# Adding up expert rows with four 64x64 tiles of TensorE: two accumulator banks, a fold by a stacked identity, and a new order of the pieces

## The reference, cut to what matters

```python
scores, pk = jax.lax.top_k(all_scores, TOPK)            # 8 experts for each token and each of 4 heads
indices = jnp.take_along_axis(all_indices, pk, axis=-1)
down = down_embed[indices]
up = up_embed[indices]
w = jnp.einsum('btd,bthkd->bthk', hidden_states, down)
w = jax.nn.silu(w) * jax.nn.softmax(scores, axis=-1)
experts_states = jnp.einsum('bthk,bthkd->btd', w, up)
mlp = jax.nn.silu(hidden_states @ Wg.T) * (hidden_states @ Wu.T) @ Wd.T
return mlp + experts_states
```

## Time and profile before

| what | value |
|---|---|
| median of 3 runs | 4052.93 us (4036.28 to 4060.89) |
| profiled execution, its own time | 4046.25 us |
| its span, first to last instruction | 4044.5 us |
| instructions | 75813 |
| mean granted TensorE clock | 0.972 of full speed |
| TensorE (PE) busy | 3814.3 us, 94% |
| VectorE (DVE) busy | 2827.7 us, 70% |
| ScalarE (ACT) busy | 2275.8 us, 56% |
| GpSimd (POOL) busy | 2242.3 us, 55% |

### The profile page before, as it was taken

How to read it: one execution, slowest core, us unless ns; L and a number is a source line. 1 busy time by engine, 2 the same in 40 slices (tenths; PEclk the granted TensorE clock), 3 DMA queues, 4 the chain that set the end, 5 groups by cost and what they waited for, 6 DMA issues and landing times.

```text
span 4044.5 us, 75813 instructions
## 1 busy us (share of the span) xinstructions
PE 3814.3 (94%) x25720; PEld 2763.9 (68%) x25720; DVE 2827.7 (70%) x9152; ACT 2275.8 (56%) x6594; POOL 2242.3 (55%) x2091
## 2 busy tenths in 40 slices
PE   7699999897679999999999999999999999999998
PEld 5577777675346777777777777777777777777766
DVE  4577787775367777777777777777777777777763
ACT  2333443343256666666666666666666666666663
POOL 1555565566266555565565565556555556556540
PEclk8899999999789999999999999999999999999999
DMA  3655555567100001000100001000010000010000
GB/s 118 154 155 144 148 154 141 153 164 201 47 1 6 7 8 35 31 12 6 39 16 27 7 6 37 17 29 4 7 39 14 29 7 27 16 31 14 5 7 27
DMA packets 110543, 210.95 MB, mean 52 GB/s; under 512 B 22321, under 2 KB 71505, under 8 KB 108625
## 3 DMA queue, kind: packets, MB, share of 16 engines
q0 software_dynamic: 40960, 134.25, 12.7%
q1 hardware_dynamic: 69056, 71.71, 5.5%
q10 hardware_dynamic: 144, 0.13, 0.0%
HBM read 191.39 MB, written 2.10 MB: 48 GB/s over the span
## 4 chain that ended last, share of the span: by engine, by line
PE 67%; issue 2%; DVE 2%; POOL 1%; ACT 1%; DMA 0%; SPq 0%; DVEq 0%; POOLq 0%; ACTq 0%
PE pj L1594 23%; PE pj L1674 12%; PE y_ps L1657 8%; PE y_ps L1683 6%; PE sc L1622 5%; PE o_ps L1648 4%; PE tp L1633 4%; PE tp L1602 4%; PE tp L1572 1%; POOL l_qk_rot L1535 1%; ACT l_probs L1753 0%; DVE l_probs L1890 0%; POOL l_r_q L1540 0%; DVE l_qk_cos L1866 0%; POOL l_r_k L1540 0%
## 5 line engine op out<-in xcount | busy, mean ns | idle before, releaser
L1594 PE MATMUL pj<-w_qkv,l_xT 128*128 128x512 f32 x2304 | 1063.1, 598 | 7.2 <-DMA l_qk_gain<-in_gains 3.6
L1535 POOL TENSOR_TENSOR l_qk_rot<-l_qk_cos,l_qk_sin 128x512 f32<-128x512 f32 x384 | 564.8, 1471 | 840.5 <-DVE l_qk_sin L1869 555.7
L382 POOL DMA_INDIRECT f_rows<-in_emb,f_expert x512 | 514.6, 1005 | 382.2 <-PE facc L601 175.0
L1594 PEld LDWEIGHTS pj<-w_qkv,l_xT 128*128 128x128 f32 x2304 | 413.5, 191 | 385.8 <-issue 375.9
L1753 ACT ACTIVATE l_probs<-l_probs,l_low 128x128 f32<-128x128 f32 x1536 | 594.0, 391 | 2.4 <-DVE l_low L1890 0.6
L1674 PE MATMUL pj<-l_xnT,l_w 128*128 128x256 f32 x2112 | 510.9, 387 | 2.2 <-issue 1.2
L1861 DVE TENSOR_REDUCE l_ss<-l_qk_sq 128x8 f32<-128x512 f32 x384 | 261.6, 681 | 324.9 <-ACT l_qk_sq L1740 173.3
L1890 DVE CUSTOM_DVE_ANT_0 l_probs<-sc,l_shut,l_r_q 128x128 f32<-128x128 f32 x1536 | 440.2, 344 | 54.4 <-PE tp L1633 46.7
L1718 ACT ACTIVATE l_qk_raw<-pj 128x512 f32<-128x512 f32 x384 | 227.0, 591 | 434.6 <-PE pj L1594 419.6
L1674 PEld LDWEIGHTS pj<-l_xnT,l_w 128*128 128x128 f32 x2112 | 383.9, 190 | 65.0 <-issue 17.4
L1657 PE MATMUL y_ps<-w_o,l_oT 128*128 128x256 f32 x1536 | 341.2, 380 | 3.5 <-ACT l_oT L1718 3.5
(11 more groups left out here) (324 smaller groups left out, 7164.6 us busy)
## 6 DMA issues: line engine op xcount, KB each, us to landing
w_qkv<-in_L_ffn_Wqkv SPq DMA_DIRECT2D x12, 1024.0 KB
l_w<-in_ff_w SPq DMA_DIRECT2D x6, 1408.0 KB, 6.1
f_rows<-in_emb,f_expert POOLq DMA_INDIRECT x512
w_o<-in_L_ffn_Wo SPq DMA_DIRECT2D x6, 1024.0 KB
w_qkv<-in_L_ffn_Wqkv SPq DMA_DIRECT2D x12, 512.0 KB
l_xf<-l_stream SPq DMA_DIRECT2D x48, 128.0 KB
l_xf<-l_stream SPq DMA_DIRECT2D x48, 127.0 KB
l_w<-in_ff_w SPq DMA_DIRECT2D x6, 768.0 KB, 4.9
```

Of the source, the lines that this page charges most:

```text
L382: pool.indirect_dma_start(rows[:, j % RH, k, :], None, dram["emb"], bass.IndirectOffsetOnAxis(ap=expert[:, n % 2, at:at + 1], axis=0)).the ...
L1535: pool.tensor_tensor(qk_rot[:, i % ROTS, :], qk_cos[:, b, :], qk_sin[:, b, :], ALU.add).then_inc(rotated if s == 0 else pool_front, 1)
L1594: last = pe.matmul(pj[b][:, :], xT[:, k, t * P:(t + 1) * P], w_qkv[:, k, s * INNER + c * 512:s * INNER + (c + 1) * 512], start=(k == 0), s ...
```

## The change

HP = 64. Each 128 tokens are two halves of 64.

- **diag** is 128x64 a slot in place of 128x128: pairs is an identity of 64x64 twice, one below the other, and c_diag (same line of code, same count) scales it. Rows 0 to 63 hold the diagonal of the first half's tokens, rows 64 to 127 that of the second's.
- **c_up** becomes eight matmuls of 64x64 by 64x256 in place of four of 128x128 by 128x256. Expert slots k and k + 1 are done together: for slot k, half i goes to output partitions of half i; for slot k + 1, to those of the other half. Half i always writes bank acc[i]. So four tiles of the array, two by rows and two by columns, have work of their own.
- **acc** is two banks, acc[0] and acc[1], and the ring has BANKS = 6.
- **c_y** becomes 16 matmuls of 128x64 by 128x256 in place of 8 of 128x128: columns for half j into acc[j].
- **c_fold** is new: ScalarE copies both banks to SBUF (two copies of 128x512, into the buffer of e_p, which now has 128 partitions), TensorE multiplies each by pairs (two matmuls of 128x64 by 128x512 into a bank of the ring), which adds each half's two parts, and VectorE's c_add takes that bank. c_y and c_up of the next batch wait for ScalarE's copies (c_copied) in place of c_add.
- GpSimd makes pairs at the start: a fill and two selects.
- **The tables** of all five engines are new.

```diff
-        ("c_up14", -5), ("c_up15", -5), ("c_m7", -4), ("c_y0", -4), ("c_up0", -4), ...
+        ("c_up15", -5), ("c_fold", -5), ("c_m7", -4), ("c_y0", -4), ("c_up0", -4), ...
...
-        ("e_ctx", -5), ("e_mask", -4), ("b_ctx", -2),
+        ("b_ctx", -1), ("e_mask", -3), ("e_ctx", -3),
...
-    BANKS = 7
+    BANKS = 6
...
+        pairs = sb("pairs", [P, HP])
...
-        diag = sb("diag", [P, 2, HALF, P])
+        diag = sb("diag", [P, 2, HALF, HP])
...
-        e_p = sb("e_p", [4 * NB, H4, SEQ])
+        e_all = sb("e_p", [P, H4, SEQ])
+        e_p = e_all[0:4 * NB, :, :]
...
+        folding = e_all[:, :, :].rearrange("p (i t) d -> p i t d", i=2)
...
-        acc = ctx.enter_context(nc.psum_tensor("facc", [P, TILES, D], F32))
+
+        acc = [ctx.enter_context(nc.psum_tensor(f"facc{i}", [P, TILES, D], F32)) for i in range(2)]
...
@@ c_y @@
-                            last = pe.matmul(acc[:, t, :], mT[:, i, t * P:(t + 1) * P], c_wd[:, i, :], ...)
+                            for j in range(2):
+                                last = pe.matmul(acc[j][j * HP:(j + 1) * HP, t, :], mT[:, i, t * P + j * HP:t * P + (j + 1) * HP], c_wd[:, i, :], ...)
...
@@ c_up @@
-                    wait(pe, c_added, n)
+                    wait(pe, c_copied, n)
...
-                    for k in range(HALF):
-                        last = pe.matmul(acc[:, j // (HALVES // TILES), :], diag[:, j % 2, k, :], rows[:, j % RH, k, D:2 * D],
-                                         start=(first and k == 0), stop=(final and k == HALF - 1))
+                    for k in range(0, HALF, 2):
+                        for s in range(2):
+                            for i in range(2):
+                                rows_at, out_at = slice(i * HP, (i + 1) * HP), slice((i ^ s) * HP, (i ^ s) * HP + HP)
+                                last = pe.matmul(acc[i][out_at, j // (HALVES // TILES), :], diag[rows_at, j % 2, k + s, :], rows[rows_at, j % RH, k + s, D:2 * D], ...)
...
+            def c_fold(n):
+                pe.wait_ge(c_copied, n + 1)
+                s = Slot("c_fold", n)
+                wait(pe, s.taken, s.before)
+                for i in range(2):
+                    last = pe.matmul(s.bank[i * HP:(i + 1) * HP, :], pairs[:, :], folding[:, i, :, :].rearrange("p t d -> p (t d)"), start=True, stop=True)
+                last.then_inc(ps_full, 1)
...
@@ ScalarE @@
-                        last = F(diag[:, j % 2, k, :], ident[:, :], ACT.Copy, scale=coef[:, j % 2, k:k + 1])
+                        last = F(diag[:, j % 2, k, :], pairs[:, :], ACT.Copy, scale=coef[:, j % 2, k:k + 1])
...
+            def c_fold(n):
+                act.wait_ge(m_used[0], n + 1)
+                act.wait_ge(m_used[1], n + 1)
+                act.wait_ge(rows_used, HALVES * (n + 1))
+                wait(act, ps_full, Slot("e_pT", n - 1).full if n > 0 else 0)
+                for i in range(2):
+                    last = F(folding[:, i, :, :], acc[i][:, :, :], ACT.Copy)
+                last.then_inc(c_copied, 1)
```

More of the change, by code:

```diff
@@ L55, in first_layers @@
     SCALE = 1.0 / 8.0
+    HP = P // 2
     ORDER = {}
     ORDER["tensor"] = [
[6 rows of a table removed]
-        ("e_s1", -5), ("c_up7", -4), ("c_up8", -4), ("a_k", -1), ("c_up9", -4), ("e_v", -5), ("e_cT", -4), ("e_pT", -5), ("a_q", -1), ("e_o", -5),
-        ("a_z", -1), ("e_y", -5), ("b_hT", -2), ("c_hT", -3), ("e_u", -5), ("c_q0", -3),
+        ("c_s0", -4), ("c_s2", -4), ("b_hT", -3), ("c_s1", -4), ("c_s3", -4), ("c_up11", -5), ("b_cT", -3), ("a_v", -2), ("c_up12", -5), ("e_k", -5),
+        ("c_m0", -4), ("c_m1", -4), ("c_m2", -4), ("c_m3", -4), ("b_g", -3), ("c_m4", -4), ("c_up13", -5), ("c_m5", -4), ("c_up14", -5), ("c_m6", -4),
+        ("c_up15", -5), ("c_fold", -5), ("c_m7", -4), ("c_y0", -4), ("c_up0", -4), ("d_hT", -5), ("a_o", -2), ("d_k", -5), ("d_q", -5), ("a_y", -2),
[3 rows of a table added]
+        ("a_q", -1), ("c_up7", -4), ("e_v", -5), ("c_up8", -4), ("c_y1", -4), ("e_pT", -5), ("c_up9", -4), ("e_o", -5), ("a_z", -1), ("e_y", -5),
+        ("c_hT", -3), ("e_cT", -4), ("e_u", -5), ("c_q0", -3), ("c_q1", -3), ("c_up10", -4),
@@ L68, in first_layers @@
     ]
     ORDER["scalar"] = [
[6 rows of a table removed]
-        ("c_diag8", -4), ("c_diag9", -4), ("b_cT", -2), ("e_exp", -5), ("e_v", -5), ("e_cT", -4), ("e_pT", -5), ("a_q", -1), ("e_o", -5),
-        ("c_tanh10", -4), ("c_diag10", -4), ("e_y", -5),
+        ("c_hT", -4), ("c_diag10", -5), ("e_cT", -5), ("c_tanh11", -5), ("c_tanh12", -5), ("c_q0", -4), ("c_diag11", -5), ("c_q1", -4),
+        ("c_tanh13", -5), ("b_cT", -3), ("c_diag12", -5), ("b_hT", -3), ("e_k", -5), ("a_exp", -2), ("a_v", -2), ("c_mtanh0", -4), ("c_diag13", -5),
[5 rows of a table added]
@@ L78, in first_layers @@
+        ("c_diag9", -4), ("e_pT", -5), ("e_o", -5), ("c_tanh10", -4), ("e_y", -5),
     ]
     ORDER["vector"] = [
[4 rows of a table removed]
[L84 to L86 removed]
@@ L361, in start @@
                 fill(zeros[:, :], 0.0)
+                fill(pairs[:, :], 0.0)
+                for at in (0, HP):
+                    pool.wait_ge(set_step, made[0])
+                    pool.affine_select(out=pairs[:, :], in_=pairs[:, :], pattern=[[-1, HP]], base=-at, channel_multiplier=1,
+                                       compare_op=ALU.not_equal, fill=1.0).then_inc(set_step, 1)
+                    made[0] += 1
                 pool.wait_ge(set_step, made[0])
@@ L589, in down @@
                         for i in chunks:
-                            last = pe.matmul(acc[:, t, :], mT[:, i, t * P:(t + 1) * P], c_wd[:, i, :], start=(first and t == 0 and i == chunks[0]),
-                                             stop=(final and t == TILES - 1 and i == chunks[-1]))
+                            for j in range(2):
+                                last = pe.matmul(acc[j][j * HP:(j + 1) * HP, t, :], mT[:, i, t * P + j * HP:t * P + (j + 1) * HP], c_wd[:, i, :],
+                                                 start=(first and t == 0 and i == chunks[0]), stop=(final and t == TILES - 1 and i == chunks[-1]), skip_group_check=True)
                     last.then_inc(m_used[half], 1)
@@ L597, in add_rows @@
                     first, final = ACC_ORDER[0] == f"c_up{j}", ACC_ORDER[-1] == f"c_up{j}"
-                    wait(pe, c_added, n)
+                    first_up = [piece for piece in ACC_ORDER if piece.startswith("c_up")][0] == f"c_up{j}"
+                    wait(pe, c_copied, n)
                     pe.wait_ge(diag_made, HALVES * n + j + 1)
-                    for k in range(HALF):
-                        last = pe.matmul(acc[:, j // (HALVES // TILES), :], diag[:, j % 2, k, :], rows[:, j % RH, k, D:2 * D],
-                                         start=(first and k == 0), stop=(final and k == HALF - 1))
+                    for k in range(0, HALF, 2):
+                        for s in range(2):
+                            for i in range(2):
+                                rows_at, out_at = slice(i * HP, (i + 1) * HP), slice((i ^ s) * HP, (i ^ s) * HP + HP)
+                                last = pe.matmul(acc[i][out_at, j // (HALVES // TILES), :], diag[rows_at, j % 2, k + s, :], rows[rows_at, j % RH, k + s, D:2 * D],
+                                                 start=((first_up if s else first) and k == 0), stop=(final and k == HALF - 2), skip_group_check=True)
                     last.then_inc(rows_used, 1)
                 return add_rows
+            def c_fold(n):
[5 more added lines that the diff above has]
+                last.then_inc(ps_full, 1)
             def d_q(n):
@@ L737, in _ @@
             do.update({f"c_up{j}": c_up(j) for j in range(HALVES)})
+            do["c_fold"] = c_fold
             do.update({"a_q": a_q, "a_k": a_k, "a_v": a_v, "a_z": a_z, "a_o": a_o, "a_y": a_y, "b_cT": b_cT, "b_g": b_g, "b_gt": b_gt,
@@ L1082, in c_m @@
                 return gate
-            def c_add(n):
-                dve.wait_ge(m_used[0], n + 1)
-                dve.wait_ge(m_used[1], n + 1)
-                dve.wait_ge(rows_used, HALVES * (n + 1))
-                x = xall[:, n, :, :]
-                V.tensor_tensor(x, acc[:, :, :], x, ALU.add).then_inc(c_added, 1)
             def d_top_(n):
```

22 lines of the change are left out of this document (13 added, 9 removed), and 35 rows, old and new, of the table ORDER.

## The result

The change measured 4082.7 us (median of 11 runs, 4067.0 to 4102.0) against 4054.0 for before (11 runs): ratio 1.0079, 95% interval 1.0064 to 1.0095. It is slower by 0.8%, where 1.4% faster was forecast, and lies above the range. The profiled execution took 4091.8 us, its span is 4090.1.

The account below looks back on a forecast made before the run. TensorE leads, with gathers, VectorE and the gather-to-c_up chain close behind. Terms sum to -7.2 us a batch, -57.6 over eight, plus 2.6 of tail: -55, giving 3998 us on the runs' footing, range 3945 to 4055.

Parts of the forecast that it names:

- c_up: TensorE's c_up matmuls: four small tiles run at once, 1.73 us becomes 1.05, 10.9 us less a batch.
- c_y: TensorE's c_y: 32 records, two tiles at once, work stays 3.46 us a piece; shape changes add 0.4 a batch.
- c_fold on TensorE: The new fold's 4 matmul records add 1.05 us of TensorE work a batch, changes of tile shape included.
- c_diag: ScalarE's diagonal copies, 64 columns shorter: 0.18 us less per four, taken as -0.5 us a batch.
- The ratio 0.65: Share of TensorE's 9.5 us saving a batch that shortens the period: -6.2 us, bounds -2.2 to -7.1.
- The wait at the accumulator: TensorE waits 1.6 us at c_fold for ScalarE's copies, replacing c_y0's 1.65 for c_add: 0, bounds -0.5 and +1.6.
- c_add later: VectorE's c_add gets its bank 2.6 us later, after copies and fold: +1.0 us a batch, bounds 0 to +2.6.
- The rest of the tables, and six banks: 0: Reordered tables and the ring's lost bank together cost nothing; bounds -3 and +3.9 us a batch.
- the context's 1.5 a batch: TensorE's wait for b_ctx's transfer mostly disappears as its load is released earlier: -1.5 us a batch, bounds 0 to -1.7.
- The ends: At the last batch nothing covers the fold, so the tail grows 2.6 us; GpSimd's setup at the start costs 0.
- the stall of TensorE's queue at c_fold: Rival: TensorE stands 1.6 us at c_fold and 3.9 at the ring: +5.9 a batch, 4103 us; chance 0.08.
- The rival of four tiles that go in turn because they accumulate: c_up's four tiles run one after another, 3.65 us each, +31 a batch, 4350 us; chance 0.03.

Follow-up runs that it names:

- h4: The change with c_fold one row later on TensorE, behind c_m7, faster kind: 3971.4 us, 0.9937 of before.
- h3: The change with whole 128x128 tiles and one accumulator, copies and fold kept, faster kind: 3996.3 us, 1.0005 of before.
- h2: Before's whole tiles, no fold, with the change's tables and six banks, faster kind: 3968.8 us, 0.9936 of before.
- h1: The change itself, unaltered, run again on the faster kind: 3958.5 us, 0.9915 of before.
- e6: Before with six banks in place of seven and nothing else, slower kind: 4065.9 us, 1.0040 of before.
- i1: Before's whole tiles, no fold, with the change's tables and six banks, slower kind: 4050.9 us, 1.0007 of before.
- e5: Before's whole tiles, no fold, with the change's tables and seven banks, slower kind: 4041.6 us, 0.9979 of before.
- f1: The change itself, unaltered, run again on the faster kind: 3958.7 us, 0.9911 of before.
- f3: The change's tiles and fold in before's tables, six banks, faster kind: 4009.4 us, 1.0046 of before.
- fourth group: Runs of before, h1, h2, h3 and h4 on one chip of the faster kind; the change took 3958.5 us there, 0.9915 of before.
- f4: The change with each c_up matmul starting its own sum, expert rows not added up, faster kind: 3961.3 us, 0.9908 of before.

## Why the prediction was wrong, step by step

- **c_up.** Right. 16 records in 1.09 us, four starting within 0.02 us and each four 0.216 to 0.27 after the four before, where I had them evenly 0.054 apart. With c_y, tiles were forecast at -10.5 us of TensorE a batch; at full clock it is -10.0 (h4 against h3).
- **c_y.** Right: 32 records in 3.67 us, two tiles at once, weight loads hidden. The rule that I weighed from the Trainium skill ("TensorE: Matmul & The Clock Gate", Part 3: Packing small matmuls) would have made it 7.9; the trace disagrees.
- **c_fold on TensorE.** 1.05 forecast, 1.5 measured at full clock. Tiles and fold together take 8.5 out at full clock (105.9 in h2, 97.4 in h1), where 9.5 was forecast.
- **c_diag.** Right: the four of a group take 1.06 us in place of 1.28, 0.21 less, where 0.18 was forecast.
- **The ratio 0.65.** Right in size where TensorE's work does fall, in the full stretches of the faster kind: h3 to h1 the period goes down 6.6 us (110.1 to 103.5) for 8.5 to 10.0 of work, 0.66 to 0.78. Over all eight batches it is 4.5 a batch: the sum took the gain of a full stretch eight times.
- **The wait at the accumulator.** The step that failed: "One wait of 1.6 takes the place of one of 1.65: 0". On the faster kind TensorE does wait 1.34, but no other wait goes away for it: period less TensorE's busy time rises from 0.7 (h2) to 2.3 (h3). On the slower kind, which the forecast was for, it waits 7.6 us. I had put 0.2 us for "the last record to get through", from no row at all; it was 5.5 to 7.7 in six of the eight batches. My bound of +1.6 lay far below. Against before, TensorE's idle time in a full stretch grew by 8.2 us (7.8 to 16.0), and some 6 of that is the wait at c_fold (7.6) less the one at c_y0 that it replaced (1.65 in four batches of five).
- **c_add later.** 2.6 forecast for the chain, 2.47 in h1; in after it is 610.05 - 600.54 = 9.5. The price of +1.0 a batch was perhaps too low even on the faster kind: h4, where c_fold and c_add come 0.5 later, is 1.6 us a batch slower than the change. That the delay is what costs it was not shown.
- **The rest of the tables, and six banks: 0.** Two effects of opposite sign. The lost bank costs 0.3 to 0.4% on the slower kind (e6; i1 less e5), 11 to 16 us in all, 1.4 to 2.0 a batch, inside my bound of +3.9. The new tables give 0.2% there, where the context's 1.5 a batch alone would be 0.3%; the two together, forecast at -1.5 a batch, come to +0.07% (i1), nothing. On the faster kind tables and bank together give 0.6% with whole tiles. With tiles and fold the tables alone give 1.35% (f1 less f3, both with six banks). Whether they suit the tiled kernel better cannot be said, since the bank's price on this kind was not measured; if it were 0.4% as on the other, 1.0% would stand against 1.35%.
- **The clock.** No term of mine held it. Around the wait of 7.48 us at c_fold the granted clock was 0.51 (605.10 to 612.00), with 1.00 on both sides; in full stretches it is 0.91 against 0.96. TensorE's busy time fell by 1.8 us there, where at full clock the same change takes 8.5 out.
- **The ends.** The last c_add comes 2.54 us after the last c_up, as forecast. I had also written that the tail would be near 55; but it is cut at c_add, so the fold cannot lengthen it, and it is 52.6, as before:

```profile
1075.04 1.62 PE L617 MATMUL facc<-f_rows,f_diag 64*64 64x256 f32 x16 [0.15 <-ACT f_diag L829]
1076.86 1.08 ACT L839 ACTIVATE f_e_p<-facc 128x512 f32<-128x512 f32 x2 [1.97 <-PE facc L617]
...
1079.20 0.69 DVE L938 TENSOR_TENSOR x_all<-fp,x_all 128x512 f32<-128x512 f32 x1 [5.41 <-PE fp L627]
```

In sum, -7.2 a batch was forecast. On the faster kind the change gives 34.8 us in the fourth group, -4.3 a batch: tables and bank -3.2, fold +3.4, tiles -4.5 (the table's per cent of 3993 us, over eight batches). On the slower kind the stretches grow by 6.4, and stay above the 116 that I had named as the sign of being wrong. Of the rivals, the stall of TensorE's queue at c_fold came nearest (4103 us, +5.9 a batch), at a chance of 0.08: right in place, near in size by luck. It had 1.6 us at c_fold, where 7.6 was seen, and 3.9 for the ring, where the bank costs 1.4 to 2.0. What held TensorE there was the late result of c_up15, which the rival did not have. The rival of four tiles that go in turn because they accumulate is refuted by the records and by f4. Two sums of mine were wrong as well. The bounds of the terms, added up, are -15.2 and +5.9 a batch, 3934 to 4103 us, and not 3965 to 4030; the wider range would have held the result. And four in turn would be +32 a batch with c_y and fold, not +37.

**What stays open.** Why results come late on one kind of chip, and why more so with small tiles. The traces of that kind also lack signals: the semaphore that counts full banks shows 397 of its 456 rises in after and 373 of 448 in before, all 456 in h1; hence "<-remote" and "<-issue" where h1 names TensorE. So the missing rises go with the kind of chip and not with small tiles. Late results would follow if records of the profile held engines up. The Trainium skill ("NOTIFIC — the notification-queue block", section 7.1, on overflow) describes such a block: it can stall what feeds it, and its inner queues hold the producer back rather than lose a record. Missing rises would not follow from that; the same section has another mode, in which a full ring discards new records. A c_up of small tiles is 32 instructions of TensorE in 1.1 us in place of 16 in 1.9. No run here tells this from another cause. The wait at c_fold is some 6 of the 8.2 us of idle time that a full stretch gained, but that its removal would bring them back was not shown: the one kernel that moved c_fold fell on the faster kind. The price of the seventh bank on the faster kind, and which rows of the tables carry their 0.6%, were not tried.

## What to carry to other kernels

Before pricing a handover at 0.2 us, measure in the trace of before how long after a matmul's last record its reader starts, place by place: here a third of the waiting gathers began late, up to 8 us after the record, and the change, which adds a handover with nothing queued in between, paid 7.6 us a batch at it. TensorE's 8.5 us less of work were worth something only where it kept its clock and was not made to stand. And run the change itself beside every variant on the same chip: two experiments looked like cures only because before and variant ran on a chip where the fault did not occur.

## What was not expected of the hardware

- Two kinds of chip, by the time of before 3992 to 3995 and 4050 to 4054 us, with a change of opposite sign on them: 0.9911 and 0.9915 against 1.0044 and 1.0079. The second stage takes the same on both (2955 us from the end of the first stage in h1, 2958 in after); nearly all of the difference is in the first, where gathers and small dependent pieces run.
- Records of TensorE that end up to 7.7 us before their reader at c_fold is let go, on the slower kind alone, and a semaphore that rises as late as they are.
- The same kernel at a granted clock of 0.91 and of 0.98 in its full stretches (after and h1), with TensorE idle for 16.0 us of a stretch in the one and 4.2 in the other.
- A fold that costs 0.69% on the kind where TensorE bounds the stage, and 0.16%, within the error, where it stands idle for 6 to 11 us a batch without it (i1).
